# A cross-attention block: both x-hat turns leave TensorE for 32 by 32 blocks on VectorE and four transfers

## The chip, the cores and the metric

The kernel runs on one core of a Trainium2 chip. The metric is the device time of that core in microseconds (us). TensorE (PE), VectorE (DVE), ScalarE (ACT) and GpSimd (POOL) each work through a list of instructions of their own, in order; SyncE (SP) issues the DMAs, in order too. Nothing but semaphores connects them.

## The reference

The inputs are x and a second sequence `memory`, both 128 sequences of 128 rows with 256 features, a mask, seven weight matrices and their biases, all float32:

```python
tgt1 = _layer_norm(tgt, g1, be1)
tgt = tgt + _self_attn(tgt1, mask, Wq, bq, Wk, bk, Wv, bv, Wo, bo)   # 16 heads of 16
tgt = tgt + (memory @ Wg.T + bg)
tgt1 = _layer_norm(tgt, g2, be2)
ff = jax.nn.relu(tgt1 @ W1.T + b1) @ W2.T + b2                       # 1024 hidden features
return tgt + ff
```

## The kernel before, in words

**Tiles.** A group is two sequences, 256 rows; there are 64 groups. The two normalised tensors (x-hat of the first layer norm, `xhat`, and of the second, `xhat2`; the second is called z) are computed with rows on the 128 partitions. Products need features on the partitions, so each is turned: TensorE multiplies four 128 by 128 tiles by an identity into a PSUM bank (`turn`, line 867). Every product is done in a reduced format three times over, from a high and a low half of both operands (`product`, lines 850 to 852). So each turned tensor is split: the high half is a rounding copy (`split_high`, on ACT; `xT[0]`, `zT[0]`), the low half a subtraction (`split_low`, line 613 on DVE, line 780 on POOL; `xT[1]`, `zT[1]`).

**Stages.** `run` unrolls 68 iterations. Iteration i does the first norm of group i+2 (`norm`), the q, k and v products of group i+1 (`front`), scores, exponentials and turned probabilities of group i (`attn_`), values, output projection and second norm of group i-1 (`out_`), and the feed-forward part of group i-2 (`ffn`). So in the middle five groups are in flight.

**Order.** It is written by hand: each engine goes through 13 ticks in every iteration, and the tuples at the top of the file say at which tick an item stands. What counts is the order in each engine's list. On TensorE, in the middle: the first two scores, the turn of the last probability chunk, the turn of x-hat and the first up product (tick 0); a score, values and q (1); a score and the second up product (2); a score, a chunk's turn and k (3); a chunk's turn and the third up product (4); scores, turns and the projection in two halves (5, 6); a score, a turn and the fourth up product (7); v (8); then turns and the four parts of the down product, with z's turn ahead of the last part (9 to 12), and the turned inverses (line 924).

**Names for the prediction.** The mask is added to each of eight chunks of scores by four fused instructions on DVE (line 651). ACT takes the exponentials (404) and copies turned probabilities (416). Up products all go to one PSUM bank: up n waits until ACT has applied relu to n-1 (446). For each of the four relu blocks DVE rounds a high half (`hT_hi`, 685), then POOL subtracts for the low half (`hT_lo`, 780), and down part n waits for low half n (`hid_split`). A layer norm is statistics on DVE (558, 565), an inverse root on POOL (773, 775), and two fused instructions on DVE that subtract the mean and multiply (573). POOL also splits `memory` (795, 780), and adds biases (808, 816). SP issues 18 DMAs in an iteration: q and k stacks (337, 343), loads, the store, and four that spread the inverse sums (375).

Of the kernel before, what the change touches and what calls it, by code (L numbers as in the profile page):

```python
# [28 lines left out]
ALU = mybir.AluOpType  # L29
# [11 lines left out]
UP_TICKS = (0, 2, 4, 7)  # L41
HIDDEN_TICKS = (1, 3, 5, 8)
RELU_TICKS = (0, 3, 5, 7)
DOWN_TICKS = (9, 10, 11, 12)
EXP_TICKS = (0, 1, 2, 3, 5, 6, 7, 9)
INVERT_TICKS = (5, 9)
# [22 lines left out]
def xattn_block(nc, x, memory, mask, wqT, wkT, wvT, woT, wgT, w1T, w2T,  # L69
# [26 lines left out]
    with ExitStack() as ctx:  # L96
# [39 lines left out]
        xhat = sb("xhat", [P, GB, D])  # L136
# [67 lines left out]
        x_turned, x_hi, x_split = sem("x_turned"), sem("x_hi"), sem("x_split")  # L204
        q_ready, q_high, q_split = sem("q_ready"), sem("q_high"), sem("q_split")
# [19 lines left out]
        z_turned, z_hi, z_split = sem("z_turned"), sem("z_hi"), sem("z_split")  # L225

        hid_ready, hid_relu, hid_hi, hid_split = (sem(f"s_hid_{n}") for n in ("ready", "relu", "hi", "split"))
        down_ready, resid_biased, y_summed = sem("down_ready"), sem("resid_biased"), sem("y_summed")

# [67 lines left out]
        def _(sp):  # L297
# [29 lines left out]
            def iteration(i, norm, front, attn_, out_, ffn):  # L327
# [21 lines left out]
                if is_at(i, GROUPS - 1):  # L349

                    sp.wait_ge(mem_split, i)
                    sp.dma_start(mem_in[:], mem_cols[i]).then_inc(mem_loaded, 16)
                if known(i, 1, GROUPS):
                    sp.wait_ge(resid_ready, i)
                    sp.dma_start(x_res[:], x_rows[i]).then_inc(xres_loaded, 16)
                if known(i, -1, GROUPS - 2):
                    sp.wait_ge(bias_ready, i + 2)
                    sp.dma_start(mask_in[:], mask_rows[i + 2]).then_inc(mask_loaded, 16)
                if known(i, -2, GROUPS - 3):
                    sp.wait_ge(ln1_ready, i + 3)  # L360
                    sp.dma_start(x_in[:], x_rows[i + 3]).then_inc(x_loaded, 16)
                if ffn:

                    sp.wait_ge(y_summed, i - 1)
                    sp.dma_start(out_rows[i - 2], y[:]).then_inc(y_stored, 16)
                if attn_:
# [5 lines left out]
                    for b in range(GB):  # L372
                        for k in range(KT):
# [3 lines left out]
                                         .broadcast_to([heads, P // heads, S])).then_inc(inv_spread, 16)  # L377

# [4 lines left out]
        def _(act):  # L383
# [8 lines left out]
            def split_high(src, dst, ready, count, free, freed, done):  # L392
# [4 lines left out]
                act.activation(dst[:], src, ACT.Copy).then_inc(done, 1)  # L397
# [28 lines left out]
            def iteration(i, norm, front, attn_, out_, ffn):  # L426
                for t in range(TICKS):
                    if out_ and t == 0:
                        copy_turned(i - 1, CHUNKS - 1)
                    if front and t == 0 and not high_by_dve(i + 1):  # L430
                        g = i + 1
                        split_high(by_tile[1], xT[0], x_turned, g + 1, v_ready,
                                   g if later(g) else None, x_hi)
                    if attn_ and t == EXP_TICKS[0]:
                        exponentials(i, 0)
                    if is_at(i, 2) and t == 0:
                        act.wait_ge(shift_added, 4)
                    if attn_ and t == 7:
                        copy_turned(i, TURN_TICKS.index(t))
# [10 lines left out]
                    if attn_ and t in TURN_TICKS and t != 7:  # L450
                        copy_turned(i, TURN_TICKS.index(t))
                    if out_ and t == 12:
                        g = i - 1
                        split_high(by_tile[1], zT[0], z_turned, g + 1, hid_ready,
                                   HJ * g if later(g) else None, z_hi)
                    if front and t == 2 and not high_by_dve(i + 1):
                        g = i + 1
                        if not later(g):
                            act.wait_ge(shift_added, 2)
                        act.wait_ge(q_ready, g + 1)  # L460
                        if later(g):
                            act.wait_ge(q_stacked, 16 * TERMS * g)
                        for k in range(KT):
                            last = act.activation(q[0][:, k, :], by_tile[1][:, k, :], ACT.Identity,
                                                  bias=bqc[:, k:k + 1])
                        last.then_inc(q_high, 1)
# [9 lines left out]
                    if attn_ and t in EXP_TICKS[1:]:  # L476
# [596 lines left out]
```

## Time and profile before

| | |
|---|---|
| three runs, median (lowest to highest) | 1755.28 us (1754.7 to 1755.63) |
| the profiled execution: device time, span | 1755.81 us, 1754.0 us |
| busy share of the span: PE, ACT, DVE, POOL | 98%, 82%, 78%, 46% |
| TensorE's granted clock | 0.8 to 0.9 of full speed in the first 5% of the span, full speed behind it |
| mean busy share of the 16 DMA engines | 33.9% (queue of the kernel's DMAs) |

The page of the profile gives the busy time of each engine and, for each group of instructions, how long it ran and how long its engine had been idle just before. A matmul is pipelined: its record is longer than the distance to the next, so what an item costs TensorE is read from one start to the next start in the timeline.

### The profile page before, as it was taken

The page shows a single profiled execution, that of the slowest core. Times are in us where ns is not written, and L with a number is a line of the kernel's source. Part 1 is how long each engine was busy: PE and PEld are TensorE (multiplying, and loading weights), DVE is VectorE, ACT ScalarE, POOL GpSimd, SP SyncE. Part 2 cuts the span into 40 slices and gives each one's busy share as a digit, 9 for nine tenths or more (in the row PEclk, how much of TensorE's full clock was granted, in tenths as well). Part 3 has the DMA queues.
Part 4 walks back from the last instruction along what each step waited for, and adds up shares of the span by engine and source line. Part 5 has one row for each costly group of instructions (what it writes and reads, how often), then busy time and mean ns, then how long its engine had stood idle before and what let it go on. Part 6 is the DMA issues. An engine that isn't in the chain of part 4 may idle for free. (4 is left out here: it accounts for less than half of the span.)

```text
span 1754.0 us, 53678 instructions
## 1 busy us (share of the span) xinstructions
PE 1724.6 (98%) x17780; PEld 1698.0 (97%) x17780; DVE 1359.8 (78%) x6945; ACT 1432.4 (82%) x5567; POOL 802.2 (46%) x782
## 2 busy tenths in 40 slices
PE   6799999999999999999999999999999999999998
PEld 6799999999999999999999999999999999999998
DVE  7777777787787777787787877877777877877874
ACT  4788888888888888888888888888888888888883
POOL 4244444444444454444444444444444444444444
PEclk8899999999999999999999999999999999999999
DMA  5333333333333332333433333333333333333320
GB/s 173 106 127 107 115 123 107 120 121 107 122 119 106 124 120 95 132 115 99 135 111 104 129 111 110 128 109 113 124 106 120 121 107 122 118 109 122 119 83 31
DMA packets 185796, 200.46 MB, mean 114 GB/s; under 512 B 18864, under 2 KB 135984, under 8 KB 185520
## 3 DMA queue, kind: packets, MB, share of 16 engines
q1 hardware_dynamic: 185520, 197.02, 33.9%
q8 instruction: 143, 2.34, 0.6%
q14 instruction: 133, 1.09, 0.2%
HBM read 62.73 MB, written 16.78 MB: 45 GB/s over the span
## 5 line engine op out<-in xcount | busy, mean ns | idle before, releaser
L404 ACT ACTIVATE scores<-scores,row_min 128x128 f32<-128x128 f32 x2048 | 795.3, 402 | 11.5 <-DVE row_min L651 11.5
L780 POOL TENSOR_TENSOR hT_lo<-hid,hT_hi 128x512 fp32r<-128x512 f32 x256 | 354.6, 1385 | 516.3 <-DVE hT_hi L685 516.3
L651 DVE CUSTOM_DVE_ANT_0 scores<-score_ps,mask_bias 128x128 f32<-128x128 f32 x2048 | 472.2, 286 | 0.9 <-issue 0.6
L416 ACT ACTIVATE probs<-turn_ps 128x512 f32<-128x512 f32 x512 | 304.8, 596 | 163.7 <-PE turn_ps L916 163.5
L404 ACT ACTIVATION_READ_ACCUMULATOR scores<-scores,row_min 128x1 f32 x2048 | 411.8, 201 | 0.0
L916 PE MATMUL turn_ps<-ident,scores 128*128 128x128 f32 x2048 | 307.6, 273 | 3.1 <-ACT probs L416 3.1
L850 PE MATMUL ffn_ps<-w_hi,hT_lo 128*128 128x256 f32 x1024 | 300.6, 294 | 0.5 <-ACT hid L446 0.5
L850 PE MATMUL ffn_ps<-zT_hi,w_lo 128*128 128x256 f32 x992 | 292.1, 294 | 0.3 <-ACT hid L446 0.3
L852 PE MATMUL ffn_ps<-w_hi,hT_hi 128*128 128x256 f32 x1024 | 284.8, 278 | 0.0
L851 PE MATMUL ffn_ps<-w_lo,hT_hi 128*128 128x256 f32 x1024 | 284.5, 278 | 0.0
L851 PE MATMUL ffn_ps<-zT_lo,w_hi 128*128 128x256 f32 x992 | 276.1, 278 | 0.0
L852 PE MATMUL ffn_ps<-zT_hi,w_hi 128*128 128x256 f32 x992 | 275.5, 278 | 0.0
L916 PEld LDWEIGHTS turn_ps<-ident,scores 128*128 128x128 f32 x2048 | 236.3, 141 | 3.5 <-ACT scores L404 3.5
L446 ACT ACTIVATE hid<-ffn_ps,vec 128x256 f32<-128x256 f32 x496 | 206.2, 469 | 0.2 <-PE ffn_ps L852 0.2
L902 PE MATMUL score_ps<-k_stack,q_stack 128*128 128x256 f32 x1024 | 201.8, 289 | 2.0 <-DVE row_min L651 1.9
L685 DVE CAST hT_hi<-hid 128x512 fp32r<-128x512 f32 x256 | 111.4, 435 | 116.5 <-ACT hid L446 116.5
L851 PEld LDWEIGHTS ffn_ps<-w_lo,hT_hi 128*128 128x128 f32 x1024 | 193.8, 189 | 0.0
L850 PEld LDWEIGHTS ffn_ps<-w_hi,hT_lo 128*128 128x128 f32 x1024 | 192.7, 188 | 0.7 <-ACT hid L446 0.7
L816 POOL TENSOR_TENSOR resid_b<-resid,row 128x512 f32<-128x512 f32 x64 | 82.2, 1284 | 241.8 <-DVE y L635 241.8
L852 PEld LDWEIGHTS ffn_ps<-w_hi,hT_hi 128*128 128x128 f32 x1024 | 192.2, 188 | 0.0
L850 PEld LDWEIGHTS ffn_ps<-zT_hi,w_lo 128*128 128x128 f32 x992 | 187.5, 189 | 0.6 <-ACT hid L446 0.5
L851 PEld LDWEIGHTS ffn_ps<-zT_lo,w_hi 128*128 128x128 f32 x992 | 187.2, 189 | 0.0
(136 smaller groups left out, 4268.4 us busy)
## 6 DMA issues: line engine op xcount, KB each, us to landing
q_stack<-q_hi SPq DMA_DIRECT2D x128, 256.0 KB, 2.4
k_stack<-k_hi SPq DMA_DIRECT2D x256, 128.0 KB, 2.3
x_in<-x_dram SPq DMA_DIRECT2D x64, 256.0 KB, 2.6
mem_in<-memory_dram SPq DMA_DIRECT2D x64, 256.0 KB, 3.0
x_res<-x_dram SPq DMA_DIRECT2D x64, 256.0 KB, 3.0
q_stack<-q_lo SPq DMA_DIRECT2D x64, 256.0 KB, 2.4
k_stack<-k_lo SPq DMA_DIRECT2D x128, 128.0 KB, 2.3
inv<-inv_cols SPq DMA_DIRECT2D x256, 64.0 KB, 2.2
```

The costliest lines, as they stand in the source:

```text
L404: last = act.activation(exps, exps, ACT.Exp, bias=row_min[:, k, h:h + 1], scale=-1.0, accum_out=row_sum[:, k, h:h + 1])
L416: act.activation(probs[:, k, :], turn_ps[k % 2][:, :], ACT.Copy).then_inc(probs_copied[k % 2], 1)
L446: last = act.activation(hid[:, n % 2, j, :], up_bank(i, n)[:, j * ROWS:(j + 1) * ROWS], ACT.Relu, bias=b1c[:, 2 * n + j:2 * n + j + 1])
L651: last = dve.tensor_tensor_reduce(out=scores[:, slot(i, t), h, :], in0=score_ps[t % 2][:, h * S:(h + 1) * S], in1=mask_bias[:, b, :], scal ...
L685: dve.tensor_copy(hT[0][:, 2 * n:2 * n + 2, :], hid[:, n % 2]).then_inc(hid_hi, 1)
L780: pool.tensor_tensor(halves[1], src, halves[0], ALU.subtract).then_inc(done, 1)
L816: pool.tensor_tensor(resid_b2[:], resid[:], b2w[:, :].unsqueeze(1).broadcast_to([P, GB, D]), ALU.add).then_inc(resid_biased, 1)
L850: pe.matmul(dst, lhs[1], rhs[0], start=start and j == 0, stop=False, **more)
L851: pe.matmul(dst, lhs[0], rhs[1], start=False, stop=False, **more)
L852: last = pe.matmul(dst, lhs[0], rhs[0], start=False, stop=stop and j == n - 1, **more)
L902: last = pe.matmul(score_ps[n % 2][:, k * 2 * S:(k + 1) * 2 * S], q_stack[i % 2][:, c, k, seq(b)], k_stack[i % 2][:, c, :, GB * k + b, :], ...
L916: last = pe.transpose(turn_ps[k % 2][:, h * S:(h + 1) * S], scores[:, slot(g, k), h, :], ident[:])
```

## The change

The turn of x-hat (from group 1 on) and that of z leave TensorE. `turn_quads` transposes 32 by 32 blocks in two VectorE instructions; it reads every fourth feature. Four DMAs of 64 KB, one for each 32 partitions, then bring the blocks to their partitions, within SBUF. x-hat is now computed in place in `x_in`, its blocks go to `x_quads` and come back to `x_in`; z's blocks go through `attn` and come back to `xhat2`. z's high half is still ACT's and its low half DVE's, from SBUF rather than PSUM. Both halves of x-hat move to POOL at tick 10, and a group's are made one iteration ahead of its q product. The x-hat of the first group is still turned on TensorE; the second group has a path of its own (`normalise_second`). On TensorE the up product of a tick now stands last in it: q, k stand at ticks 0 and 2, up at 1, 3, 5 and 7, behind the values. The other engines' lists follow, and `inv` is spread ahead of the store of y. The diff, cut to its core:

```diff
-UP_TICKS = (0, 2, 4, 7)
-HIDDEN_TICKS = (1, 3, 5, 8)
-RELU_TICKS = (0, 3, 5, 7)
+UP_TICKS = (1, 3, 5, 7)
+HIDDEN_TICKS = (4, 5, 6, 8)
+RELU_TICKS = (3, 4, 5, 7)
...
-EXP_TICKS = (0, 1, 2, 3, 5, 6, 7, 9)
-INVERT_TICKS = (5, 9)
+EXP_TICKS = (0, 1, 2, 3)
+INVERT_TICKS = (6, 9)
...
+            return w[:].rearrange("p b (k c j) -> p b k j c", j=QUADS, c=32)
...
+            return w.rearrange("p (j k b r) -> p b k j r", j=QUADS, k=KT, b=GB)
...
+                if norm and i + 2 > 0:
+
+                    sp.wait_ge(x_blocked, i + 2)
+                    for n in range(QUADS):
+                        sp.dma_start(x_flat[:, n * P:(n + 1) * P],
+                                     x_blocks[32 * n:32 * (n + 1), :].rearrange("c (j n) -> c j n", j=QUADS)
+                                     ).then_inc(x_cols, 16)
...
+                if out_:
+
+                    sp.wait_ge(z_blocked, i)
+                    for n in range(QUADS):
+                        sp.dma_start(xhat2_flat[:, n * P:(n + 1) * P],
+                                     attn_blocks[32 * n:32 * (n + 1), :].rearrange("c (j n) -> c j n", j=QUADS)
+                                     ).then_inc(z_cols, 16)
...
+                    if attn_ and t in (4, 6, 7, 9):
+                        exponentials(i, CPB + (4, 6, 7, 9).index(t))
+                    if out_ and t == 12:
+                        g = i - 1
+                        split_high(quad_cols(xhat2), in_order(zT[0]), z_cols, 16 * QUADS * (g + 1), hid_ready,
+                                   HJ * g if later(g) else None, z_hi)
...
+                dve.wait_ge(ready, count)
+                for b in range(GB):
+                    last = dve.transpose(quad_blocks(dst)[:, b], quad_rows(src)[:, b])
+                last.then_inc(done, 1)
...
-                    if attn_ and t in INVERT_TICKS:
+                    if ffn and t == 0:
+                        g = i - 2
+                        dve.wait_ge(z_hi, g + 1)
+                        dve.tensor_tensor(in_order(zT[1]), quad_cols(xhat2), in_order(zT[0]), ALU.subtract
+                                          ).then_inc(z_split, 1)
...
+                    if ffn and t in HIDDEN_TICKS and t < 8:
+                        hidden_high(i - 2, HIDDEN_TICKS.index(t))
...
+                    if norm and t == 5 and i >= 0:
+                        layer_norm_apply(i + 2, x_in, mv1, rstd1, ln1_rstd, x_in, ln1_ready)
+                        dve.wait_ge(x_cols, 16 * QUADS * (i + 1))
+                        turn_quads(x_blocks, x_in, ln1_ready, i + 3, x_blocked)
+                    if out_ and t == 8:
+                        g = i - 1
+                        if later(g):
+                            dve.wait_ge(z_split, g)
+                        layer_norm_apply(g, resid, mv2, rstd2, ln2_rstd, xhat2, ln2_ready)
+                        dve.wait_ge(attnT_split, g + 1)
+                        turn_quads(attn_blocks, xhat2, ln2_ready, g + 1, z_blocked)
+                    if ffn and t == HIDDEN_TICKS[-1]:
+                        hidden_high(i - 2, HJ - 1)
...
+                    if norm and t == 5:
+                        inverse_root(i + 2, mv1, var1, rstd1, ln1_mean, ln1_var, ln1_ready, ln1_rstd)
...
+                    if norm and i >= 0 and t == 10:
+                        g = i + 2
+                        pool.wait_ge(x_cols, 16 * QUADS * g)
+                        pool.wait_ge(v_ready, g)
+                        pool.tensor_tensor(in_order(xT[0]), quad_cols(x_in),
...
+                        pool.tensor_tensor(in_order(xT[1]), quad_cols(x_in), in_order(xT[0]), ALU.subtract
+                                           ).then_inc(x_pool_split, 1)
...
-                    if front and t == 0:
-                        pe.wait_ge(ln1_ready, i + 2)
-                        if not isinstance(i, int) or outs > 0:
-                            pe.wait_ge(z_split, outs)
-                        turn(by_tile[1], xhat).then_inc(x_turned, 1)
-                    if ffn and t in UP_TICKS:
-                        up(i, t)
...
-                    if front and t in (1, 3):
+                    if front and t in (0, 2):
                         which = t // 2
                         if which == 0:
-                            pe.wait_ge(x_split, i + 2)
+                            if i < 1:
+                                pe.wait_ge(x_split, i + 2)
+                            else:
+                                pe.wait_ge(x_pool_split, i)
...
-                    if out_ and t == (11 if i == GROUPS else 12):
-                        pe.wait_ge(ln2_ready, i)
-                        pe.wait_ge(resid_ready, i)
-                        turn(by_tile[1], xhat2).then_inc(z_turned, 1)
+                    if ffn and t in UP_TICKS:
+                        up(i, t)
```

## Rows read from the trace of the kernel before

**Rows 1.** A window: PE, PEld, DVE, ACT, POOL busy us (count), PE clock, DMA.

```profile
800.00:1000.00 200.00, 200.00 (x2065) 197.73 (x2064) 157.36 (x823) 169.40 (x664) 93.66 (x92) 1.00 0.35 115
```

**Rows 2.** Once an iteration: turned inverses; count, ns min/median/max, first and last start.

```profile
L924 PE MATMUL turn_ps<-ident,sum_inv x49: 270/270/270, 422.8 to 1696.4; 128*128 128x128 f32 x49
```

**Rows 3.** Timeline of PE: start, us, engine, line, op, tiles; first instructions of blocks.

```profile
1004.25 0.60 PE L916 MATMUL turn_ps<-ident,scores 128*128 128x128 f32 x4
1004.69 0.60 PE L867 MATMUL work_ps<-ident,xhat 128*128 128x128 f32 x4
1005.04 0.36 PE L850 MATMUL ffn_ps<-w_hi,hT_lo 128*128 128x256 f32 x1
...
1006.57 0.72 PE L902 MATMUL score_ps<-k_stack,q_stack 128*128 128x256 f32 x4
1007.13 0.60 PE L916 MATMUL turn_ps<-ident,scores 128*128 128x128 f32 x4
1007.56 0.60 PE L867 MATMUL work_ps<-ident,xhat 128*128 128x128 f32 x4
1007.92 0.37 PE L850 MATMUL ffn_ps<-zT_hi,w_lo 128*128 128x256 f32 x1
...
1009.38 0.39 PE L902 MATMUL score_ps<-k_stack,q_stack 128*128 128x256 f32 x2
1009.70 1.96 PE L940 MATMUL value_ps<-probs,v_pad 128*32 128x128 f32 x64
1011.58 0.38 PE L850 MATMUL work_ps<-xT_hi,wq_lo 128*128 128x256 f32 x1
...
1013.10 0.40 PE L902 MATMUL score_ps<-k_stack,q_stack 128*128 128x256 f32 x2
```

**Rows 4.** Timeline of DVE in the same iteration, first instructions of its items.

```profile
1012.33 0.69 DVE L675 TENSOR_TENSOR attn<-value_ps,inv 128x512 f32<-128x512 f32 x1
...
1016.77 0.69 DVE L613 TENSOR_TENSOR attnT_lo<-attn,attnT_hi 128x512 fp32r<-128x512 f32 x1
1017.37 0.87 DVE L702 SCALAR_TENSOR_TENSOR q_lo<-work_ps,qk_bias,q_hi 128x256 fp32r<-128x256 f32 x2
1018.17 0.29 DVE L651 CUSTOM_DVE_ANT_0 scores<-score_ps,mask_bias 128x128 f32<-128x128 f32 x1
...
1020.08 0.56 DVE L583 RECIPROCAL sum_inv<-row_sum 128x32 f32<-128x32 f32 x2
1020.63 0.43 DVE L685 CAST hT_hi<-hid 128x512 fp32r<-128x512 f32 x1
1020.97 0.87 DVE L714 SCALAR_TENSOR_TENSOR k_lo<-work_ps,qk_bias,k_hi 128x256 fp32r<-128x256 f32 x2
...
1022.78 0.06 DVE L648 MEMSET carrier<- 128x1 f32 x1
...
1023.99 0.69 DVE L623 TENSOR_TENSOR resid<-work_ps,x_res 128x512 f32<-128x512 f32 x1
...
1026.89 0.88 DVE L573 SCALAR_TENSOR_TENSOR xhat<-resid,mv,rstd 128x256 f32<-128x256 f32 x2 [0.20 <-POOL rstd L775]
```

**Rows 5.** Timeline of DVE: a copy that reads with a stride.

```profile
8.39 0.61 DVE L506 COPY hid<-inv 128x512 f32<-128x512 f32 x1
```

**Rows 6.** Timeline of both engines where VectorE's pair meets two POOL instructions.

```profile
25.30 6.16 DVE L573 SCALAR_TENSOR_TENSOR xhat<-x_in,mv,rstd 128x256 f32<-128x256 f32 x2
...
26.48 4.69 POOL L762 TENSOR_TENSOR w_lo<-probs,w_hi 128x2048 fp32r<-128x2048 f32 x1
```

**Rows 7.** POOL's groups, 400 to 1600 us: busy us, mean ns | idle before.

```profile
L780 POOL TENSOR_TENSOR memT_lo<-mem_in,memT_hi 128x512 fp32r<-128x512 f32 x46 | 62.3, 1354 | 3.6
...
L795 POOL TENSOR_TENSOR memT_hi<-mem_in,one 128x512 fp32r<-128x512 f32 x46 | 48.0, 1044 | 0.0
```

**Rows 8.** SP's timeline: four transfers of the new ones' shape.

```profile
1007.94 2.57 SPq L375 DMA_DIRECT2D inv<-inv_cols  x4
```

**Rows 9.** The page's DMA issues: count, KB each, median us to landing.

```profile
inv<-inv_cols SPq DMA_DIRECT2D x256, 64.0 KB, 2.2
```

More of the change, by code:

```diff
@@ L429, in iteration @@
                         copy_turned(i - 1, CHUNKS - 1)
[L430 to L433, printed above, removed]
+                    if is_at(i, -1) and t == 0:
+                        split_high(by_tile[1], xT[0][:], x_turned, 1, v_ready, None, x_hi)
                     if attn_ and t == EXP_TICKS[0]:
@@ L437, in iteration @@
                         act.wait_ge(shift_added, 4)
+                    if front and t == 1 and not high_by_dve(i + 1):
+                        g = i + 1
+                        if not later(g):
+                            act.wait_ge(shift_added, 2)
+                        act.wait_ge(q_ready, g + 1)
+                        if later(g):
+                            act.wait_ge(q_stacked, 16 * TERMS * g)
+                        for k in range(KT):
+                            last = act.activation(q[0][:, k, :], by_tile[1][:, k, :], ACT.Identity,
+                                                  bias=bqc[:, k:k + 1])
+                        last.then_inc(q_high, 1)
                     if attn_ and t == 7:
+                        copy_turned(i, TURN_TICKS.index(t))
+                    if attn_ and t == 5:
                         copy_turned(i, TURN_TICKS.index(t))
@@ L449, in iteration @@
                         last.then_inc(hid_relu, 1)
-                    if attn_ and t in TURN_TICKS and t != 7:
+                    if attn_ and t in EXP_TICKS[1:]:
+                        exponentials(i, EXP_TICKS.index(t))
+                    if attn_ and t in TURN_TICKS and t not in (5, 7):
                         copy_turned(i, TURN_TICKS.index(t))
[L452 to L466, printed above, removed]
                     if front and t == 3 and not high_by_dve(i + 1):
@@ L608, in high_part, with hidden_high @@
                 last.then_inc(early_high, 1)
+            def hidden_high(g, n):
+                dve.wait_ge(hid_relu, HJ * g + n + 1)
+                if n == 0 and later(g):
+                    dve.wait_ge(down_ready, g)
+                dve.tensor_copy(hT[0][:, 2 * n:2 * n + 2, :], hid[:, n % 2]).then_inc(hid_hi, 1)
             def split_low(src, halves, high, count, done):
@@ new lines, in iteration @@
+                    if is_at(i, -1) and t == 0:
+                        split_low(by_tile[1], xT, x_hi, 1, x_split)
+                    if is_at(i, 0) and t == 0:
+                        dve.wait_ge(x_cols, 16 * QUADS)
+                        dve.wait_ge(v_ready, 1)
+                        dve.tensor_copy(in_order(xT[0]), quad_cols(x_in)).then_inc(early_high, 1)
+                        dve.wait_ge(early_high, 1)
+                        dve.tensor_tensor(in_order(xT[1]), quad_cols(x_in), in_order(xT[0]), ALU.subtract
+                                          ).then_inc(x_split, 1)
@@ L686, in iteration @@
+                    if attn_ and t in INVERT_TICKS and t < 9:
+                        invert_sums(i, INVERT_TICKS.index(t))
                     if is_at(i, -1) and t == 1:
@@ L688, in iteration @@
                         dve.wait_ge(shift_added, 2)
[L689 to L694 removed]
+                    if front and t == 2:
                         g = i + 1
```

147 lines of the change are left out of this document (86 added, 61 removed).

## The prediction

> **What bounds the kernel now.** First the window of the middle [rows 1]: TensorE is busy for 200.00 of 200 us at full granted clock (1.00, the level of 2.4 GHz), VectorE for 157, ScalarE for 169, POOL for 94. The reader is to see that no gap is left on TensorE, so that in the middle a wait removed is worth nothing and only work taken off TensorE's list can shorten it. Then the period: 49 turned inverses, one in an iteration, from 422.8 to 1696.4 us, so 1273.6 / 48 = 26.53 us for an iteration [rows 2]. Third, what each item costs TensorE: in its timeline, from a block's start to the next one's [rows 3].
>
> **What is taken off TensorE.** A chunk's turn followed by z's turn starts at 1004.25, z's at 1004.69, the next product at 1005.04. The pair takes 0.79; one turn ahead of a product takes 0.35, so one saved is 0.44. For x-hat: 1007.13, 1007.56, 1007.92, and 0.79 - 0.36 = 0.43 [rows 3]. Together 0.87 us of 26.53. The longer first product behind a float32 turn stays, since in both places another turn stands ahead. If TensorE stays without gaps, the period is 25.66 us. The order of up, q and k among themselves changes no instruction; it costs nothing as long as no wait ends late.
>
> **What is put on the others.** VectorE gets four transposes of 128x256, two for each tensor, and loses x-hat's low half (0.60 from start to start, as the low half of 1016.77 to 1017.37 [rows 4]). No row shows such a transpose. The nearest are the pairs of float32 instructions of 128x256 elements: 0.80 from the pair's start to the next item's (1017.37 to 1018.17) and 0.88 to its end [rows 4]. I take 0.80 for a pair of transposes. From below I bound it by two thirds of that, 0.53, since one input is read, not two. From above: a copy of 128x512 that reads in strides takes 0.61 us [rows 5], where the plain rounding copy of as many elements takes 0.43 [rows 4], so 0.18 more. These new reads take every fourth feature. With 0.18 on each a pair is 1.16.
> The Trainium skill (SBUF — State Buffer, The DMA port swizzle) says that SBUF has lines of 16 bytes and that an access which goes to a new line each time pays a penalty; a step of four float32 is just such a step, so the rule speaks against this change. By it the pair would be at the upper bound, by the pairs in the trace at 0.80; the strided copy agrees that strides can cost, but not that they do at one element a cycle.
>
> ScalarE loses x-hat's high half and keeps the rest, 169 of 200 us before [rows 1]. POOL gets both halves of x-hat: 1.04 and 1.35 by the two halves of memory [rows 7]; 94 of 200 us busy becomes some 113. SP gets eight issues. Four of this very shape take 2.57 us to issue [rows 8] and land 2.2 us later [rows 9], so z's columns are there about 4.2 us after the block turn (three issues of 0.64, then 2.2). They are needed only at the next iteration's values, so in the middle TensorE doesn't see them. On SP's own list both fours stand behind waits that end anyway in that order (x-hat's behind k's stack, z's behind the load of x_res), and inv now goes ahead of the store.
>
> **Where VectorE and POOL meet.** Behind rounding the second relu block (tick 5) VectorE has x-hat's pair of fused instructions, and that rounding is what releases POOL's subtraction of 1.3 us. At 25.30 the trace shows what happens then: the pair lasts 6.16 us, because after its first half POOL's instruction of 26.48 runs for 4.69 and only then the second half [rows 6]. Both read two SBUF operands. So VectorE and POOL take turns, instruction by instruction. In the old order that pair met an idle POOL. In the new one POOL's subtraction falls between the halves: the pair ends 0.35 (the first half, a little under 0.40) + 1.28 (POOL, between 1.04 and 1.35 [rows 7]) + 0.3 (31.46 - 31.17, what the second half needs behind POOL's end [rows 6]) = 1.93 after its start rather than 0.88, so 1.05 lost on VectorE. From below the loss is nothing, if the second half goes ahead of POOL.
> The Trainium skill (SBUF — State Buffer, SBUF: two separate sides) states this as a lock on a shared pair of ports for a whole instruction; the trace agrees.
>
> **The loop that decides.** The fourth relu block's rounding is now behind nearly all of VectorE's list, and two things hang on it: the last down part (through POOL's low half), and x-hat's halves on POOL, which now stand behind that low half. Both are due just ahead of the next q. That q leads, through values and the first up product, to the fourth score pair, and that pair starts VectorE's list anew. I add it up.
> - TensorE, q to the fourth pair: q 1.52, a pair 0.32, values 1.88, up 1.46 (1007.92 to 1009.38): 5.18 [rows 3]. The pair's scores reach VectorE 0.55 later (0.40 of the record and an estimated 0.15 for the signal).
> - VectorE from there, by starts [rows 4]: five mask chunks at 0.90 (two in 1018.17 to 1020.08, with a small wait), of which one is inside the stretch below; attn 0.70; rounding four times at 0.34 (1020.63 to 1020.97), the last 0.42 to its end; the low half of attn 0.60; k's low half and x-hat's statistics 1.81 (1020.97 to 1022.78); x-hat's pair 0.88; inverse sums 0.55; the stretch residual, statistics, mask chunk, wait for the root 2.90 (1023.99 to 1026.89); z's pair 0.88. With 4 x 0.90 and 3 x 0.34 + 0.42 + 0.34 this is 13.70. Two pairs of transposes add 1.60, the meeting with POOL 1.05: 16.35.
> - POOL and back: signal 0.08, low half 1.35, signal 0.07, last down part 1.53 (1005.04 to 1006.57), two score pairs and a turn 0.99 (1006.57 to 1007.56) [rows 3, 7]: 4.02. By the other way, x-hat's halves 1.04 + 1.35 in place of 1.53 + 0.99, it is nearly the same.
>
> Sum 5.18 + 0.55 + 16.35 + 4.02 = 26.10 us. That is above TensorE's 25.66, so the loop sets the period and TensorE stands idle for some 0.4 us in each iteration. Other waits come out in time by the same adding: the second up product waits for the first relu, with some 0.4 to spare, and the projection for attn's low half, 0.6.
>
> **Ends.** In the first iterations and in the last, z's and the second x-hat's way is not covered: block turn 0.8 and 4.2 for the transfers against 0.35 on TensorE, so at most 4.6 each; in the tail the last down parts cover some. I take 5 us in all (0 to 9).
>
> **Forecast.** About 62 full iterations: (26.53 - 26.10) x 62 = 27 us saved, 5 lost at the ends: 1755.8 - 22 = 1734 us. The sum is made against the profiled execution's 1755.81 (span 1754.0), which stands 0.5 us above the median of the runs.
>
> **Rivals.**
> 1. *TensorE stays the bound.* If the loop is 0.44 shorter than I add it (the transposes at 0.53 a pair give 0.54, or POOL's subtraction waits until the pair is over: 1.05), the period is 25.66: 0.87 x 62 = 54 saved, 5 lost: 1707. For it: each of twenty terms is a little rounded up. Against it: rows 6.
> 2. *The strided block turn is slow* (the rule of lines above, and the slower side). At 1.16 a pair the loop is 26.82: 0.29 x 62 = 18 more and 5 at the ends: 1779. It decides from 0.97 a pair on (26.45 us, where the saving no longer pays the ends). The same side is reached if POOL reads x-hat's runs of 32 elements slower than memory's whole rows: by the ratio 0.61 to 0.43 its two halves take 1.0 more, and the loop through them 27.1.
> 3. *It just cancels*: pairs near 0.97, 1752 to 1759.
>
> That TensorE keeps the turns is no rival: the only turn of x-hat left in its list is the first group's.
>
> **How the numbers follow.** The forecast (loop at 25.8 to 26.35, 1715 to 1751) has 0.40, TensorE bound (1700 to 1715) 0.20, the slower side 0.30, cancelling 0.10. Within 0.2% (3.5 us) is what a measurement of this kernel can't tell from no change. Faster 0.60, same 0.10, slower 0.30. For 8 in 10 I leave out the fastest tenth and the slowest: 1703 to 1781.
>
> **What would show it.** Right: a period of about 26.1 by the turned inverses; idle time of PE ahead of the last down part or of q, released by POOL's hT_lo or xT_lo; a transpose of about 0.45 to 0.5 us by record; x-hat's pair (now written to x_in) lasting about 1.9 us with POOL's hT_lo between its halves. Rival 1: PE busy 200 of 200 and 25.66. Rival 2: a transpose of over 0.6 by record, or POOL's xT instructions far above 1.35. The prediction is wrong altogether if PE waits elsewhere, for relu (ScalarE held up by z's columns) or for scores.

## The result and the profile after

The changed kernel takes 1759.08 us (median of 20 runs, 1757.0 to 1761.59) where the kernel before takes 1755.24 in runs on the same chip: ratio 1.0024, interval 1.0017 to 1.003. That is slower, by about as much as a measurement of this kernel can tell. The forecast was 1734 us and a clear gain: its range holds the time, its side is wrong.

First the window of the middle, in the columns of [rows 1]:

```profile
800.00:1000.00 200.00, 196.52 (x2016) 192.53 (x2017) 176.42 (x838) 165.93 (x664) 109.30 (x105) 1.00 0.43 137
```

TensorE now stands idle for 3.5 of 200 us, at full granted clock as before. VectorE went from 157 to 176 us, POOL from 94 to 109. The turned inverses, which [rows 2] gave for before:

```profile
L1030 PE MATMUL turn_ps<-ident,sum_inv x49: 273/273/273, 424.8 to 1693.1; 128*128 128x128 f32 x49
```

(1693.1 - 424.8) / 48 = 26.42 us an iteration, where before took 26.53: the 0.87 us taken off TensorE's list gave 0.11. The waits of the middle (400 to 1600 us: who waited for whom, us in total, times, longest) say where the rest is:

```profile
ACT zT_hi L441 <- DMA xhat<-attn: 105.2, 46, 3.5
...
PEld ffn_ps L956 <- POOL hT_lo L874: 34.7, 45, 1.1
...
PE ffn_ps L956 <- POOL hT_lo L874: 24.0, 45, 0.8
```

In each iteration TensorE waits ahead of the last down part for POOL's low half of the fourth relu block, where the forecast had put the wait. (ScalarE's wait for z's columns is the longest of the three; onez, below, tests whether it costs anything.) One such place in TensorE's timeline, then POOL's and VectorE's over the same iteration (start, length, and in brackets the idle time before):

```profile
1003.82 0.60 PE L1022 MATMUL turn_ps<-ident,scores 128*128 128x128 f32 x4
1005.08 0.38 PE L956 MATMUL ffn_ps<-w_hi,hT_lo 128*128 128x256 f32 x1 [0.65 <-POOL hT_lo L874]
...
1006.57 0.27 PE L1030 MATMUL turn_ps<-ident,sum_inv 128*128 128x128 f32 x1
...
1007.51 0.38 PE L956 MATMUL work_ps<-xT_hi,wq_lo 128*128 128x256 f32 x1
```

```profile
1003.75 1.28 POOL L874 TENSOR_TENSOR hT_lo<-hid,hT_hi 128x512 fp32r<-128x512 f32 x1 [2.64 <-DVE hT_hi L684]
1004.98 1.09 POOL L918 TENSOR_TENSOR xT_hi<-x_in,one 128x512 fp32r<-128x512 f32 x1
1006.15 1.30 POOL L923 TENSOR_TENSOR xT_lo<-x_in,xT_hi 128x512 fp32r<-128x512 f32 x1
...
1020.07 1.47 POOL L874 TENSOR_TENSOR hT_lo<-hid,hT_hi 128x512 fp32r<-128x512 f32 x1 [0.67 <-DVE hT_hi L684]
```

```profile
1013.21 0.06 DVE L722 MEMSET carrier<- 128x1 f32 x1 [1.27 <-PE score_ps L1008]
...
1019.57 0.42 DVE L684 CAST hT_hi<-hid 128x512 fp32r<-128x512 f32 x1
1019.91 1.92 DVE L617 SCALAR_TENSOR_TENSOR x_in<-x_in,mv,rstd 128x256 f32<-128x256 f32 x2
1021.93 1.17 DVE L626 STREAM_TRANSPOSE x_quads<-x_in 128x256 f32<-128x256 f32 x2
...
1028.57 1.16 DVE L626 STREAM_TRANSPOSE attn<-xhat 128x256 f32<-128x256 f32 x2
1029.66 0.39 DVE L684 CAST hT_hi<-hid 128x512 fp32r<-128x512 f32 x1
```

The reader is to see four things. TensorE's wait costs more than its idle time shows: from the chunk's turn to the down part it is 1.26 us (1003.82 to 1005.08), where the same two stand 0.35 apart when nothing is waited for (1025.37 and 1025.72 in the same timeline), so 0.91 is lost. From the fourth pair of scores, at which VectorE starts again behind a wait (1013.21), its list runs nearly without a gap to the fourth rounding, which ends at 1030.05. X-hat's pair takes 1.92 us and POOL's 1.47 lies inside it. And each pair of transposes takes 1.16 to 1.17 us. By groups, over 400 to 1600 us (times | busy us, mean ns | idle before):

```profile
L617 DVE SCALAR_TENSOR_TENSOR x_in<-x_in,mv,rstd 128x256 f32<-128x256 f32 x90 | 86.0, 996 | 0.0
...
L626 DVE STREAM_TRANSPOSE x_quads<-x_in 128x256 f32<-128x256 f32 x90 | 53.1, 632 | 4.7
L626 DVE STREAM_TRANSPOSE attn<-xhat 128x256 f32<-128x256 f32 x90 | 52.4, 620 | 4.7
```

The loop, added up anew from this iteration: q to the fourth pair of scores 5.18 (1007.51 to 1012.69), to VectorE 0.56 (its first mask instruction starts at 1013.25), VectorE's list 16.80 (to 1030.05), POOL and back to q 3.84 (1003.67, where the fourth rounding of this round ends, to 1007.51). Sum 26.38, within 0.04 of the mean period. Both ways back tie: xT_lo ends at 1007.45 and q, which the last down part reaches without a gap, starts at 1007.51. VectorE's list ahead of 1013.21 is not in the loop: there it waits 1.27 us for the scores.

**The ends.** 0.11 x 62 iterations is 6.8 us won in the middle, yet the span is 3.3 us longer (1757.3 against 1754.0), so the ends lost 10.1. TensorE's timeline of the tail, of the changed kernel and then of the kernel before:

```profile
1717.48 0.27 PE L1030 MATMUL turn_ps<-ident,sum_inv 128*128 128x128 f32 x1
...
1736.73 0.38 PE L956 MATMUL ffn_ps<-w_hi,hT_lo 128*128 128x256 f32 x1 [1.23 <-POOL hT_lo L874]
1741.12 0.38 PE L956 MATMUL score_ps<-zT_hi,w_lo 128*128 128x256 f32 x1 [2.74 <-DVE zT_lo L733]
```

```profile
1719.69 0.27 PE L924 MATMUL turn_ps<-ident,sum_inv 128*128 128x128 f32 x1
...
1736.09 0.66 PE L867 MATMUL work_ps<-ident,xhat 128*128 128x128 f32 x4 [0.62 <-DVE xhat L573]
```

From the last turned inverse to the end of the span it is 1757.3 - 1717.48 = 39.8 us, before 34.3: 5.5 lost. The two waits shown are 3.97 us, where before has 0.62. The other large part is TensorE's clock. Just behind the wait of 2.74 us its granted clock falls to half (0.50, the level of 1.2 GHz; the last column but two of the window):

```profile
1743.00:1745.00 2.00, 2.00 (x12) 2.00 (x11) 0.43 (x1) 0.84 (x2) 0.30 (x1) 0.50 0.00 0
```

From 1742.16 to 1745.57 sixteen products start 0.21 us apart rather than 0.11, which costs 1.6 us. The kernel before has full clock here. The kernel of meet, below, has the same two waits (1.26 and 2.74) but full clock behind them, and its stretch is 38.2 us, 1.6 shorter. Why the clock fell in one and not in the other no run shows.

The iteration ahead of the last turned inverse is 1.1 us longer than before's (1693.1 to 1717.48 against 1696.4 to 1719.69). In the start the second turned inverse stands at 53.26 in both kernels, the third at 77.87 instead of 76.15, behind a wait of 4.96 us for the inverse sums, which VectorE reaches later; at 424.8 the kernel is 2.0 behind although some 13 full iterations should have won 1.4. That is 3.5. Here too a part is the clock: behind the wait of 4.96 us q takes 2.70 us (79.71 to 82.41) where it takes 1.47 in the middle, at a granted clock of 0.50 (window 78 to 82 us). The kernel before has half clock in its start as well, so how much of the 3.5 this is stays open.

### The profile page after: what moved, and what is told of

Its sections match the earlier page's. It is cut to its first block and busy times, and to the rows that moved or that the text cites. A ratio compares the mean times of both kernels' runs of the same rounds, so it can differ in the third digit from the quotient of the medians.

```text
span 1757.3 us, 53486 instructions
## 1 busy us (share of the span) xinstructions
PE 1684.2 (96%) x17272; PEld 1643.0 (93%) x17272; DVE 1509.3 (86%) x7136; ACT 1393.1 (79%) x5506; POOL 953.5 (54%) x906
## 5 line engine op out<-in xcount | busy, mean ns | idle before, releaser
L874 POOL TENSOR_TENSOR hT_lo<-hid,hT_hi 128x512 fp32r<-128x512 f32 x256 | 339.6, 1327 | 687.7 <-DVE hT_hi L684 687.7
L448 ACT ACTIVATION_READ_ACCUMULATOR scores<-scores,row_min 128x1 f32 x2048 | 420.5, 205 | 0.0
L1008 PE MATMUL score_ps<-k_stack,q_stack 128*128 128x256 f32 x1024 | 206.7, 294 | 2.3 <-DVE row_min L725 2.3
L958 PEld LDWEIGHTS ffn_ps<-zT_hi,w_hi 128*128 128x128 f32 x992 | 186.3, 188 | 0.0
L725 DVE DVE_READ_ACCUMULATOR2_ANT row_min<- 128x1 f32 x2048 | 168.9, 82 | 0.0
```

Source lines behind the costliest of these rows:

```text
L448: last = act.activation(exps, exps, ACT.Exp, bias=row_min[:, k, h:h + 1], scale=-1.0, accum_out=row_sum[:, k, h:h + 1])
L725: last = dve.tensor_tensor_reduce(out=scores[:, slot(i, t), h, :], in0=score_ps[t % 2][:, h * S:(h + 1) * S], in1=mask_bias[:, b, :], scal ...
L874: pool.tensor_tensor(halves[1], src, halves[0], ALU.subtract).then_inc(done, 1)
L958: last = pe.matmul(dst, lhs[0], rhs[0], start=False, stop=stop and j == n - 1, **more)
L1008: last = pe.matmul(score_ps[n % 2][:, k * 2 * S:(k + 1) * 2 * S], q_stack[i % 2][:, c, k, seq(b)], k_stack[i % 2][:, c, :, GB * k + b, :], ...
```

## Experiments

All are made from the changed kernel. The periods come from the turned inverses, as above. Each ratio is against the kernel before, run on the same chip; its median was between 1754.86 and 1755.52 us there, so times of different experiments can be compared within about 2 us.

**meet: the meeting of VectorE and POOL alone.** The second rounding, which releases POOL's subtraction, goes between x-hat's pair and its block turn.

```diff
-                    if ffn and t in HIDDEN_TICKS and t < 8:
+                    if ffn and t in HIDDEN_TICKS and t < 8 and t != 5:
...
                         layer_norm_apply(i + 2, x_in, mv1, rstd1, ln1_rstd, x_in, ln1_ready)
+                    if ffn and t == 5:
+                        hidden_high(i - 2, 1)
+                    if norm and t == 5 and i >= 0:
                         dve.wait_ge(x_cols, 16 * QUADS * (i + 1))
```

> One edit of the changed kernel: on VectorE the rounding of the second relu block moves from ahead of x-hat's pair (the two fused instructions that write x_in) to between that pair and its block turn. Theory (VectorE and POOL take turns at instructions with two SBUF operands; the loop from the fourth score pair through VectorE's list to the last hT_lo on POOL and back to q sets the period): the pair falls from 1.92 to 0.88 us, the loop from 26.42 to about 25.4, so TensorE is the bound again at 25.66, PE busy near 200 of 200 us, and 0.76 x 62 = 47 us are saved: 1712 us. Rival (the pair is slow because it writes over its own input): it stays at 1.92 and the time at 1759. Rival (POOL's subtraction now meets the block turn): the turn's pair grows from 1.16 to over 2 and the time stays near 1759.

1710.06 us, ratio 0.9746 (0.9733 to 0.9759). X-hat's instructions in the middle, then the window of 200 us:

```profile
L617 DVE SCALAR_TENSOR_TENSOR x_in<-x_in,mv,rstd 128x256 f32<-128x256 f32 x94 | 41.3, 481 | 0.0
```

```profile
800.00:1000.00 200.00, 200.00 (x2112) 197.33 (x2111) 174.24 (x880) 172.75 (x685) 112.75 (x109) 1.00 0.46 142
```

996 ns an instruction became 481, so 1.03 us left the loop. TensorE has no gap left, the period is (1669.0 - 415.2) / 49 = 25.59 us. Both rivals are out: the pair still writes over its own input and takes 0.88 us, and the block turn beside which POOL's subtraction now runs stays at 622 ns an instruction. One line's place in a list is worth 49 us here.

**contig: the price of the stride alone.** The block turn reads 32 neighbouring features instead of every fourth; the weights' rows and the vectors are loaded in the matching order.

```diff
-            return w[:].rearrange("p b (k c j) -> p b k j c", j=QUADS, c=32)
+            return w[:].rearrange("p b (k j c) -> p b k j c", j=QUADS, c=32)
...
+                        sp.dma_start(to[:, m, :], src[m * P:(m + 1) * P, :].rearrange("(j c) n -> c j n", j=QUADS)
+                                     ).then_inc(weight_loaded[name], 16)
```

> The block turn reads 32 neighbouring features in place of every fourth one; the rows of Wq, Wk, Wv and W1 and the entries of g1, be1, g2 and be2 are loaded to the partitions that this asks for (one more DMA for each of the four, one more for the vectors), and the first group's x-hat is written in that order. Nothing else of the changed kernel is altered. Theory (the stride is what makes a transpose 0.63 us by record): a transpose falls to 0.45 to 0.48, a pair from 1.10 to 0.8 from start to start, the loop by 0.6 to 25.8 us, 0.6 x 62 = 37 saved, 1 to 2 us more at the start: about 1723. Rival (a float32 transpose takes this long whatever the stride): 0.63 stays and the time is 1759 to 1761.

1715.12 us, ratio 0.9775 (0.9762 to 0.9789), period (1672.2 - 413.4) / 49 = 25.69:

```profile
L624 DVE SCALAR_TENSOR_TENSOR x_in<-x_in,mv,rstd 128x256 f32<-128x256 f32 x94 | 90.0, 999 | 0.0
L633 DVE STREAM_TRANSPOSE x_quads<-x_in 128x256 f32<-128x256 f32 x94 | 36.3, 424 | 4.9
L633 DVE STREAM_TRANSPOSE attn<-xhat 128x256 f32<-128x256 f32 x94 | 36.3, 424 | 5.0
```

A transpose of 128x256 float32 takes 0.42 us from neighbouring elements and 0.62 to 0.63 at a step of 16 bytes; the pair's meeting with POOL is untouched (999 ns). So the stride cost 0.8 us of the loop (0.2 in each of four instructions), and that alone also decides. The expectation, 1723 us, had put it at 0.6.

**both: the two together.**

> Both edits: the rounding of the second relu block between x-hat's pair and its block turn, and block turns that read neighbouring features. Theory: the loop is at 24.8 us, a good 0.8 below TensorE's own list, so the period is 25.66 us and the time 1712 to 1714, the same as with the first edit alone within some 2 us. Rival (another loop, for example ScalarE's through z's columns, lies just below): a period between 25.7 and 26.4 and PE waiting for relu or for exponentials.

1709.25 us, ratio 0.9742 (0.9728 to 0.9755), period (1667.6 - 414.5) / 49 = 25.57, TensorE busy for 200.00 of 200 us. Either cure gets nearly everything, together they get no more: behind the loop stands TensorE's own list, at 25.57 to 25.59 where the forecast's floor was 25.66.

**onez: z's transfers.** Only one of z's four is made (three quarters of z's columns are left out of the computation).

```diff
-                    for n in range(QUADS):
+                    for n in range(1):
```

> The changed kernel with one of z's four transfers (the other three left out, so three quarters of z's columns are not turned; the waits count one). Theory (the loop through POOL's hT_lo): ScalarE's wait for z's columns (2.3 us an iteration) ends 1.9 us earlier, the period stays at 26.42, only the tail is some 2 us shorter: 1757. Rival (ScalarE, held up by z's columns, delays relu and the exponentials and through them TensorE): the period falls towards 25.66 and the time towards 1712.

1755.22 us, ratio 1.0002 (0.9994 to 1.0011), period (1692.1 - 424.5) / 48 = 26.41. ScalarE's wait for z's columns fell from 105.2 to 13.2 us over 400 to 1600 us, the biggest wait after POOL's, and TensorE's waits for hT_lo stayed at 35.0 and 24.3. So that long wait cost nothing in the middle. Of the 3.9 us that the time did fall, 0.01 x 62 = 0.6 is the period and the rest the ends, where nothing covers z's way.

**fourth: the fourth rounding ahead of z's block turn.** This takes one pair of transposes out of the deciding loop in another way. It missed.

```diff
                         layer_norm_apply(g, resid, mv2, rstd2, ln2_rstd, xhat2, ln2_ready)
-                        dve.wait_ge(attnT_split, g + 1)
-                        turn_quads(attn_blocks, xhat2, ln2_ready, g + 1, z_blocked)
                     if ffn and t == HIDDEN_TICKS[-1]:
                         hidden_high(i - 2, HJ - 1)
+                    if out_ and t == 8:
+                        dve.wait_ge(attnT_split, g + 1)
+                        turn_quads(attn_blocks, xhat2, ln2_ready, g + 1, z_blocked)
```

> One edit of the changed kernel: on VectorE the rounding of the fourth relu block stands ahead of z's block turn (behind z's fused pair) and not behind it. Strides and x-hat's pair are as in the changed kernel. Theory (the loop): the block turn's 1.10 us leave the stretch ahead of POOL's last low half, the loop goes from 26.42 to about 25.3, TensorE is the bound: period 25.6, about 1710 us; a transpose stays at 0.63 and x-hat's pair at 1.92. Rival (ScalarE's chain from z's columns, now 0.3 us later, is nearly as long): a period of 25.8 to 26 and PE waiting for relu.

1750.4 us, ratio 0.9969 (0.9959 to 0.9979), period (1685.1 - 422.5) / 48 = 26.30. The waits of the middle, from 400 to 1600 us, hold no hT_lo on TensorE any more:

```profile
ACT zT_hi L441 <- DMA xhat<-attn: 97.4, 45, 4.0
...
DVE zT_lo L733 <- ACT zT_hi L441: 21.8, 44, 2.3
PEld ffn_ps L957 <- ACT hid L501: 17.7, 46, 0.4
```

In their place TensorE waits for relu, in each iteration, as the forecast's last paragraph feared; and 40 times ahead of the values, 14.8 us on its weight loads, for something that the profile doesn't name. In ScalarE's list the last copy of turned probabilities, which the values need, stands right behind z's high half, so z's columns may hold up both; the second part of that is argued from the order alone. ScalarE's list shows why (exponentials left out, as the other lines between):

```profile
1002.58 0.63 ACT L441 ACTIVATE zT_hi<-xhat 128x512 fp32r<-128x512 f32 x1 [2.04 <-DMA xhat<-attn]
1003.12 0.26 ACT L468 ACTIVATE inv_cols<-turn_ps 128x128 f32<-128x128 f32 x1
...
1005.29 0.82 ACT L488 ACTIVATE q_hi<-work_ps,qk_bias 128x256 fp32r<-128x256 f32 x2
...
1009.09 0.82 ACT L501 ACTIVATE hid<-ffn_ps,vec 128x256 f32<-128x256 f32 x2
```

ScalarE waits for z's columns and from then on has no gap until relu, whose end lets the second up product go. By this reading there is a second loop, and it goes round once in two iterations: fourth score pair (1007.37) through VectorE's list to the end of z's block turn (1024.67) 17.3 us, columns, ScalarE and the second up product 11.5, TensorE's list from there to the fourth score pair of the next iteration 23.6. Sum 52.4, or 26.2 an iteration. Added up in the changed kernel, without TensorE's wait for hT_lo, it is 17.0 + 11.6 + 23.5 = 52.1, so 26.05: hidden some 0.4 us below the first loop.

**fourth_onez: the second loop put to the test.** The edits of fourth and onez together (with onez's part of the computation left out).

> Changed kernel with the fourth relu block's rounding ahead of z's block turn, and only one of z's four transfers (three quarters of z's columns are left out of the computation). Theory (fourth missed because of a second loop, through z's columns and ScalarE's list, which takes two iterations for 52.4 us): three issues of 0.64 us less on SP take 1.9 us out of it, so (52.4 - 1.9) / 2 = 25.25 us, below TensorE's floor of 25.6; the period is then 25.6 us and the time about 1710 us (1707 to 1714), TensorE busy for 200 of 200 us. Rival (the miss lies in the transposes or in ScalarE's work itself, not in z's columns being late): the period stays at 26.3 us and the time at 1750 us. Alone, the leaving out of three transfers had changed nothing (1.0002).

1705.33 us, ratio 0.9714 (0.9701 to 0.9727), period (1667.4 - 414.0) / 49 = 25.58:

```profile
800.00:1000.00 200.00, 200.00 (x2112) 197.33 (x2111) 181.07 (x871) 173.36 (x684) 113.38 (x110) 1.00 0.42 135
```

Alone, leaving out three transfers had moved the period by 0.01 us; with the first loop out of the way it moves it by 0.72, and the time by 45 us. Fourth missed because of z's columns, then. The meeting with POOL and the slow transposes are both still in this kernel.

**fourth_contig.**

> Changed kernel with both the fourth rounding ahead of z's block turn and the block turn reading 32 neighbouring features. Theory: the second loop holds both pairs of transposes and z's columns once in each iteration; each pair is 0.4 us shorter, so it is 26.2 - 0.4 to 26.2 - 0.8 = 25.4 to 25.8 us, TensorE's floor is 25.57: period 25.6 to 25.8, time 1710 to 1721 us. Rival (ScalarE's own list bounds it, whatever VectorE does): 26.2 us and 1746 us.

1716.43 us, ratio 0.978 (0.9766 to 0.9793), period (1677.0 - 417.1) / 49 = 25.71. The second loop shrinks with the transposes as well, so it isn't ScalarE's list by itself. It is no better than contig alone.

**meet_more and both_more: how much room is left.** X-hat's block turn is done twice, first into a spare tile that nobody reads, with a wait behind each instruction. One run adds this to meet, the other to both.

```diff
+                        for b in range(GB):
+                            dve.transpose(x_spare[:].rearrange("p b (k j c) -> p b k j c", k=KT, j=QUADS)[:, 0],
+                                          quad_rows(x_in)[:, b]).then_inc(spare_set, 1)
+                            dve.wait_ge(spare_set, GB * i + b + 1)
```

> The kernel of the first edit (second rounding behind x-hat's pair) with more work on VectorE: x-hat is block-turned once more, to a spare tile that nobody reads, two strided transposes with a wait behind each, about 0.71 us each. Theory: the loop was at 26.42 - 1.04 = 25.38, 0.2 below TensorE's 25.59; with 1.42 more it is 26.8, so 1.2 x 62 = 75 us more than that kernel: about 1785. Rival (slack that was not seen, more than 1 us): under 1730.

1767.0 us, ratio 1.0069 (1.0053 to 1.0084), period (1676.4 - 402.0) / 48 = 26.55. From VectorE's timeline:

```profile
1026.72 1.31 DVE L810 STREAM_TRANSPOSE x_spare<-x_in 128x256 f32<-128x256 f32 x2
1028.06 1.19 DVE L628 STREAM_TRANSPOSE x_quads<-x_in 128x256 f32<-128x256 f32 x2
```

The extra pair took 1.34 us. TensorE's waits for hT_lo are back (40.3 us in 46 on its weight loads). So the loop of meet is 26.55 - 1.34 = 25.21 us, 0.38 below TensorE's list; from the changed kernel's it should be 26.42 - 1.03 = 25.39, and 0.18 of that I can't place. The expectation was 18 us too high: those 0.18 in 62 iterations are 11 of them, and the extra pair was 0.08 shorter than assumed, another 5.

> The kernel with both edits and the same extra block turn, here of neighbouring features, about 0.50 us for each transpose with its wait. Theory: the loop was at 24.56 (25.38 less four times 0.205), a full 1.0 below TensorE's 25.57; with 1.0 more it is 25.6 and just covered: 1709 to 1715. Rival (VectorE's time costs one for one wherever it is added): 1.0 x 62 = 62 more, about 1771.

1712.87 us, ratio 0.9759 (0.9745 to 0.9772), period (1671.5 - 415.4) / 49 = 25.63. With both cures there is room for a third pair of transposes at 0.06 us an iteration.

**z_on_pe and z_on_pe_early: half of the change.** Z's turn goes back to TensorE, x-hat's stays with the blocks.

```diff
-                        turn_quads(attn_blocks, xhat2, ln2_ready, g + 1, z_blocked)
...
+                    if out_ and t == (11 if i == GROUPS else 12):
+                        pe.wait_ge(ln2_ready, i)
+                        pe.wait_ge(resid_ready, i)
+                        turn(by_tile[1], xhat2).then_inc(z_turned, 1)
```

> Changed kernel with z turned on TensorE again (as in the kernel before, ahead of the last down part; no block turn and no transfers for z), x-hat's turn still by blocks. Theory: one turn goes back to TensorE, floor 25.59 + 0.44 = 26.03 us; the loop through VectorE and POOL loses one pair of transposes, 26.42 - 1.17 = 25.25 us, so TensorE is the bound again, busy for 200 of 200 us, period 26.0 us. The end costs nothing, the start some 4 us: 1755.8 - (26.53 - 26.03) x 62 + 4 = 1729 us (1725 to 1733). Rival (the loss in the changed kernel hangs on x-hat's side alone, the fused pair's meeting with POOL and x-hat's columns): the period stays at 26.4 us and the time at about 1750 us.

1827.13 us, ratio 1.0402 (1.0388 to 1.0416), period (1680.5 - 409.9) / 46 = 27.62. That is 98 us over the expectation, since the edit brought a wait of its own (VectorE's timeline):

```profile
1017.67 0.69 DVE L702 TENSOR_TENSOR y<-ffn_ps,resid_b 128x512 f32<-128x512 f32 x1 [2.05 <-PE ffn_ps L948]
...
1019.13 0.69 DVE L726 TENSOR_TENSOR zT_lo<-work_ps,zT_hi 128x512 fp32r<-128x512 f32 x1
```

Z's low half stands behind y and a mask chunk, and q, which writes over that PSUM bank, behind it. With blocks nothing in PSUM is held, so this place was free; with the turn it costs 1.6 us in each iteration (27.62 - 26.03, with the next run). The next run has it ahead of y, as in the kernel before:

> As z_on_pe, z turned on TensorE, but with z's low half at its place of the kernel before, ahead of the sum y. In z_on_pe it stood behind y and the first mask chunk, and q, which writes the PSUM bank of z's turn, waited for it: 1.3 and 1.5 us in each iteration (period 27.6 us), so that run said nothing of z's share. Theory: that wait goes (z's low half ends about 1.6 us behind z's turn, q is due 2.8 us behind it); TensorE's floor is 25.59 + 0.44 = 26.03 us, the loop through VectorE and POOL 26.42 - 1.17 = 25.25 us; TensorE busy for 200 of 200 us, period 26.0 us, time 1729 us (1725 to 1733). Rival (the loss of the changed kernel hangs on x-hat's side alone): period 26.4 us, about 1750 us, with TensorE waiting for POOL's hT_lo.

1728.98 us, ratio 0.9853 (0.9837 to 0.987):

```profile
L1019 PE MATMUL turn_ps<-ident,sum_inv x50: 270/270/270, 418.5 to 1694.1; 128*128 128x128 f32 x50
```

(1694.1 - 418.5) / 49 = 26.03 us with TensorE busy for 200.00 of 200: one turn costs TensorE 26.03 - 25.59 = 0.44 us, the forecast's figure. The half change is 30 us faster than the whole: 0.39 x 62 = 24 by the period, the rest at the ends. The second turn takes 0.44 off TensorE and puts 1.17, a pair of transposes, into VectorE's loop.

**tail: the end alone, and the best version.** Meet, and the last group's z turned on TensorE.

```diff
+                    if is_at(i, GROUPS) and t == 11:
+                        pe.wait_ge(ln2_ready, i)
+                        pe.wait_ge(resid_ready, i)
+                        turn(by_tile[1], xhat2).then_inc(z_turned, 1)
```

> The kernel of the first edit, and the last group's z is turned on TensorE as in the kernel before (its halves from PSUM, no transfers). Theory (at the end nothing covers the block turn and the four transfers): TensorE's idle 2.7 us ahead of the last up products goes, less about 0.4 for the turn: 1707 to 1708 against 1710. Rival (another chain of the tail is as late): no change.

1705.66 us, ratio 0.9719 (0.9706 to 0.9732). From the last turned inverse to the end it is 1702.8 - 1667.06 = 35.7 us where meet takes 1707.2 - 1668.99 = 38.2, so the edit is worth 2.5 us, as expected. The time fell by 4.4, but the two profiled executions are already 2.7 apart at their first turned inverse behind 400 us, where the edit changes nothing. This version is 50 us faster than the kernel before, and nearly all of that is meet: the change with one rounding moved behind x-hat's pair.

## Why the prediction was wrong, step by step

- **TensorE's savings: right.** The floor was forecast at 25.66 us and is 25.57 to 25.59. Z's turn is worth 0.44 (26.03 - 25.59), as forecast. The rest of the change, x-hat's turn and the new order, is worth 26.53 - 26.03 = 0.50, where the forecast had 0.43 for the turn and nothing for the order; part of that is q, which takes 1.47 instead of 1.52.
- **The transposes: this is the step that failed.** The forecast took 0.80 us for a pair; by record a pair takes 1.16 to 1.17. The upper bound, built from the strided copy of [rows 5], was 1.16, and contig shows that it is the stride: 0.42 an instruction without, 0.62 to 0.63 with. The 0.18 by which that copy is slower was nearly the size (0.20). I went by the nearest pair in the trace because no row showed a stride slowing an instruction other than that copy. But a pair without stride isn't evidence on a stride; the strided copy was the only row that was. Two pairs at 0.36 too little are 0.72 us of a loop whose whole margin was 0.43. (By starts, as the forecast counted, a pair takes 1.11 and 1.09, but VectorE pauses 0.10 ahead of each, which the forecast left out: 1.20 in all.) The Trainium skill (SBUF — State Buffer, The DMA port swizzle) says that an access which takes a new 16-byte line each time pays a penalty. Contig agrees with that, by the 0.42 and 0.62 above, and the rule should have weighed more than it did.
- **The meeting with POOL: right.** 1.93 forecast, 1.92 measured; by meet it is 1.03 us an iteration and 49 us of time. It was in the forecast at its full price, so it is not why the forecast failed.
- **The loop: right in kind, 0.40 too long in the rest.** With the measured transposes the forecast's sum is 26.10 + 0.72 = 26.82, rival 2's. Measured 26.42 (26.38 in the iteration added up). VectorE's list is 0.27 shorter than that sum (17.07 against 16.80; the mask chunks run at 0.85, not 0.90), POOL and the way back 0.18 (3.84 against 4.02: the low half 1.28, the down part 1.49). These small roundings up hid more than half of the missing 0.72. So rival 2 had the mechanism, and its 1779 us was 20 too many: 25 too many by the period, 5 too few at the ends. The other way to rival 2, POOL slowed by the runs of 32 elements, didn't come: its halves take 1.09 and 1.30 us.
- **The ends: mis-sized.** 5 us (0 to 9) forecast, 10.1 measured, outside that range: 5.5 in the tail, 3.5 in the start, 1.1 in the iteration ahead of the last turned inverse. The sum allowed at most 4.6 for z's way in the tail. It had no term for TensorE's clock, which took 1.6 there, and none for z's low half, which takes 1.30 us there where before it took 0.69.
- **Together.** The time is 25 us over the forecast: (26.42 - 26.10) x 62 = 20 by the loop, 5 by the ends. With 5 us at the ends it would have been 1754, about the same as before. So the transposes took the gain, and the ends decided the sign. That the time lies in the range of 8 in 10 is no merit of the sum: too cheap a transpose and too dear a rest offset each other in part.
- **"Other waits come out in time": right for this kernel, but not added far enough.** The loop through z's columns and ScalarE was some 0.4 us below the first (fourth, fourth_onez). The text said of z's columns that they are needed only at the next iteration's values, so that TensorE doesn't see them. That held (onez), but only while the first loop was the longer one: behind z's columns stands the wait for relu.

## What to carry over

Work taken off the bound engine is worth only the distance to the next loop: add that loop up with the price of the added instructions at its upper bound, and if the sign of the result hangs on which bound is right, give both signs nearly the same chance. When a step is added to an engine's list, look at what each line there releases: moving one rounding behind a pair that reads two SBUF operands was worth 49 us, and the change as first written gained nothing. A cure that takes only the first loop away shows the second, so before claiming its gain add up the next wait on every engine, over two iterations if a tensor is used an iteration later. And where a change leaves TensorE waiting in the start or the tail, look at its granted clock there too.

## What the runs showed of the hardware

A float32 transpose of 32 by 32 blocks, 128x256, took 0.42 us from neighbouring elements and 0.62 to 0.63 with a step of four floats, so the step costs half as much again.

Two fused VectorE instructions that read and write SBUF, with a POOL subtraction of two SBUF operands released between them, took 1.92 us instead of 0.88, and POOL's went from 1.28 to 1.47. Z's low half shows the same. Before, it read one operand from PSUM and took 0.69 us in each of 45 iterations of the middle. In the changed kernel both lie in SBUF, POOL adds a bias beside it, and it takes 1.22 (median of 46):

```profile
1007.61 1.29 POOL L910 TENSOR_TENSOR resid_b<-resid,row 128x512 f32<-128x512 f32 x1 [0.15 <-DVE y L709]
...
1008.23 1.22 DVE L733 TENSOR_TENSOR zT_lo<-xhat,zT_hi 128x512 fp32r<-128x512 f32 x1
```

In z_on_pe, with the PSUM operand back and the same addition of POOL beside it (1018.50 to 1019.77), it took 0.69 again (1019.13, shown above). This costs the changed kernel nothing in the middle, since it falls ahead of VectorE's wait of 1.27 us. A block transpose, which reads one SBUF operand, wasn't slowed in meet (1.17 us at 1018.14, with POOL's subtraction from 1018.30 to 1019.60). But the mask's bias, which reads one SBUF tensor too, took 0.79 us at 1004.38 beside POOL's subtraction and 0.23 at 1002.95 before, when POOL had only instructions of two columns. That looks like the same meeting; it wasn't tried by itself.

Four transfers of 64 KB within SBUF took 2.48 us to issue, and z's high half began 4.07 us behind the end of the block turn (1003.36 to 1007.43), where the forecast had 4.2.

TensorE's granted clock fell to half (0.50) for 3.4 us in the tail of the changed kernel, just behind a wait of 2.74 us, and products of 128x256 then started 0.21 us apart instead of 0.11. In the same place of meet, behind the same wait, it did not fall.
